# Two-layer transformer block on one core: normalisation by halves of the tokens, a new order of layer 1's first steps, and products on TensorE whose results nobody reads

## The reference

```python
x = L0_attn_x
xn = _layernorm(x, axis=-1)
s = _L0_attn_ref(xn, ...)          # 16 heads of 16, rope, degree-4 polynomial attention, out projection
g = _silu(_L0_ffn_ref(xn, ...))    # 4-bit weights unpacked, gate/up 2048, gelu, down
x = x + s * g
xn = _layernorm(x, axis=-1)
s = _L1_attn_ref(xn, ...)          # 16 q heads and 4 kv heads of 128, rope, alibi, capped softmax
g = _silu(_L1_ffn_ref(xn, ...))    # router, top 4 of 32 experts, one shared expert
x = x + s * g
```

## Time and profile before

| | before |
|---|---|
| three runs, us | 869.6, 869.14, 864.97 (median 869.14) |
| profiled execution, us | 866.74, its span 865.0 |
| busy: PE, DVE, ACT, POOL | 779.7 (90%), 612.7 (71%), 465.6 (54%), 422.8 (49%) |
| PE busy, in 40 slices of 21.6 us | 2999999988788758898999899999999999999996 |
| granted clock of PE in the same slices | 9999999999998989988999999999999999999999 |

### The profile page before, as it was taken

One profiled execution on the slowest core, in us unless ns is written; L12 is line 12 of the kernel. 1 busy time (PEld: TensorE's weight loads), 2 busy tenths in 40 slices (PEclk: granted clock), 3 DMA queues, 4 the chain that ended last, 5 costly groups with the idle time before them and its releaser, 6 DMA issues.

```text
span 865.0 us, 13854 instructions
## 1 busy us (share of the span) xinstructions
PE 779.7 (90%) x4835; PEld 635.0 (73%) x4835; DVE 612.7 (71%) x1063; ACT 465.6 (54%) x819; POOL 422.8 (49%) x478
## 2 busy tenths in 40 slices
PE   2999999988788758898999899999999999999996
PEld 2876776764223237687988788989999999988884
DVE  8388869547988868788877886767766654445555
ACT  3433342259888823676645556556566555655431
POOL 2566846423554454454433357577663412665430
PEclk9999999998989988999999999999999999999999
DMA  5111186000000040000000001110110569644107
GB/s 180 38 53 57 38 243 179 1 1 1 1 1 2 1 143 6 26 7 7 25 7 13 7 26 50 44 37 32 56 50 1 197 128 346 218 146 106 48 4 241
DMA packets 50115, 59.81 MB, mean 69 GB/s; under 512 B 13559, under 2 KB 41084, under 8 KB 50048
## 3 DMA queue, kind: packets, MB, share of 16 engines
q1 hardware_dynamic: 45488, 50.49, 19.2%
q0 software_dynamic: 4560, 8.44, 2.7%
HBM read 41.11 MB, written 21.86 MB: 73 GB/s over the span
## 4 chain that ended last, share of the span: by engine, by line
PE 56%; DVE 12%; POOL 6%; ACT 6%; issue 4%; DMA 1%; POOLq 0%; ACTq 0%; DVEq 0%; SPq 0%
PE ps L771 12%; PE ps L515 8%; PE ps L517 7%; PE ps L516 7%; PE ps L864 4%; PE ps L861 3%; PE ps L895 3%; POOL A L1735 2%; DVE cap L1442 2%; DVE swap L1432 2%; PE ps L609 2%; PE ps L554 2%; PE ps L843 2%; PE ps L686 2%; PE ps L780 1%
## 5 line engine op out<-in xcount | busy, mean ns | idle before, releaser
L1105 ACT ACTIVATE cap<-cap 128x1024 f32<-128x1024 f32 (+7 forms) x128 | 87.1, 680 | 123.1 <-DVE cap L1442 123.1
L771 PE MATMUL ps<-V,P 128*128 128x129 f32 x1152 | 152.6, 279 | 0.0
L771 PEld LDWEIGHTS ps<-V,P 128*128 128x128 f32 x1152 | 145.2, 194 | 2.7
L1442 DVE SCALAR_TENSOR_TENSOR cap<-dist,ps 128x1024 f32<-128x1024 f32 (+7 forms) x128 | 95.1, 749 | 26.2 <-PE ps L517 21.4
L1661 POOL TENSOR_SCALAR_AFFINE_SELECT P<-P 128x128 f32<-128x128 f32 x128 | 38.6, 301 | 148.8 <-ACT P L1110 148.5
L1791 POOL DMA_INDIRECT y_scratch<-y_sb,aux_s x63 | 62.0, 984 | 61.6 <-ACT y_sb L1150 40.3
L1110 ACT ACTIVATE P<-cap 128x1024 f32<-128x1024 f32 (+7 forms) x128 | 87.7, 685 | 4.1
L515 PE MATMUL ps<-q_hi,k_hi 128*128 128x512 f32 x192 | 72.1, 376 | 6.9 <-DVE cap L1442 6.2
L517 PE MATMUL ps<-q_lo,k_hi 128*128 128x512 f32 x192 | 67.0, 349 | 0.0
L516 PE MATMUL ps<-q_hi,k_lo 128*128 128x512 f32 x192 | 66.8, 348 | 0.0
L1766 POOL TENSOR_TENSOR rot<-rot,swap 128x512 f32<-128x512 f32 x40 | 52.1, 1304 | 19.7 <-DVE swap L1432 19.5
(11 more groups left out here) (288 smaller groups left out, 2099.2 us busy)
## 6 DMA issues: line engine op xcount, KB each, us to landing
xg_scratch<-blank SPq DMA_DIRECT2D x1, 8127.0 KB, 32.5
xa<-xg_scratch SPq DMA_DIRECT2D x63, 128.0 KB, 2.2
ew<-in_experts SPq DMA_DIRECT2D x3, 1920.0 KB, 8.7
y<-y_scratch SPq DMA_DIRECT2D x8, 512.0 KB, 5.4
pk<-in_packed SPq DMA_DIRECT2D x8, 384.0 KB, 3.2
pks<-in_scales SPq DMA_DIRECT2D x8, 384.0 KB, 4.0
ew<-in_experts SPq DMA_DIRECT2D x1, 3072.0 KB, 12.9
wqk<-in_wqk SPq DMA_DIRECT2D x20, 128.0 KB, 2.0
```

What stands on the lines that cost most here:

```text
L771: last = pe.matmul(ps[:, 4 + r % 2, o:o + D1 + 1], P1[:, h % 2, a:a + P], V1[:, j, h // REP, :], start=(j == 0), stop=(j == t))
L1105: act.activation(cap[:, n % 2, 0:w], cap[:, n % 2, 0:w], ACT.Tanh, scale=1.0 / (CAP * float(D1) ** 0.5))\
L1442: dve.scalar_tensor_tensor(out=cap[:, n % 2, 0:w], in0=dist[:, 0:w], scalar=slope, in1=psf[:, 1024 * (n % 2):1024 * (n % 2) + w], op0=ALU. ...
```

## The change

- Both layers: square root, `rsqrt`, shift and normalisation run for tiles 0 to 3, then for tiles 4 to 7. In each half DVE normalises two tiles and ACT two. `transpose_x`, `layernorm_hi` and `layernorm_lo` run by halves, in other PSUM banks.
- Layer 0: half 0 is normalised after the statistics of tile 4. wqkv is split by chunk on ACT and POOL, and POOL starts only after `shift_ready` of half 0. The second half's transposes stand between tiles 1 and 2 of `qkv0`; `nibbles(0, ...)` on DVE moves behind tile 0's copy, `halves(0)` behind tile 1's and the second half's low parts.
- Layer 1: DVE normalises half 0 between the statistics of tiles 4 and 5. POOL's `split_wqk(1)` and the router's split move behind wv's. The list begins: k0 half 0, values 0 and 1, the second half's transposes, q0 half 0, values 2 and 3, k0 half 1, q0 half 1, values 4 to 7. On ACT the high part of k0 half 0 comes after the second half's high parts.
- `keep_clock(n, bank)`: n products of x_tok with itself (128x128 by 128x256, 32-bit) into a bank that nobody reads. Eight once x's first half has landed, two after the first transposes of layer 0; six and two at the same places of layer 1.

```diff
+XT_BANKS = [(0, 2), (2 * PAIR_OF["turn_o", 1], OUT_BANKS[2])]
-            def transpose_x(layer):
-                for k in range(2 * NHALF):
-                    half, c = k // NC, k % NC
-                    pe.wait_ge(xn_ready if half == 0 else xn_act_ready, 4 * layer + 4)
+            def transpose_x(layer, half):
+                pe.wait_ge(xn_ready, 4 * layer + 2 * half + 2)
+                pe.wait_ge(xn_act_ready, 4 * layer + 2 * half + 2)
+                for c in range(NC):
                     for i in range(4):
...
             def qkv0():
-                pe.wait_ge(wqkv_ready, 1)
                 for t in range(NT):
+                    if t == 2:
+                        transpose_x(0, 1)
...
+                            if t == 0:
+                                pe.wait_ge(wqkv_ready, c + 1)
...
+            def keep_clock(n, bank):
+                for _ in range(n):
+                    pe.matmul(ps[:, bank, 0:D], x_tok[:, 0, 0:P], x_tok[:, 0, :], start=True, stop=True)
+
+            pe.wait_ge(in_x[0], 16)
+            keep_clock(8, 7)
             pe.wait_ge(in_const, 32)
-            transpose_x(0)
+            transpose_x(0, 0)
+            keep_clock(2, 7)
             qkv0()
...
-            pe.wait_ge(x_ready, NT)
-            transpose_x(1)
+            keep_clock(6, 2 * PAIR_OF["turn", H0 // QUAD - 1])
+            transpose_x(1, 0)
+            keep_clock(2, 2 * PAIR_OF["turn", H0 // QUAD - 1])
...
         def _(act):
...
+            layernorm_sd(0, 0)
             act.wait_ge(in_const, 32)
-            act.activation(wqkv_hi[:], wqkv[:], ACT.Copy).then_inc(wqkv_hi_ready, 1)
-            layernorm_sd(0)
-            layernorm_norm(0)
-            layernorm_hi(0)
+            split_wqkv(0)
+            layernorm_norm(0, 0)
+            split_wqkv(1)
+            layernorm_hi(0, 0)
+            layernorm_sd(0, 1)
+            layernorm_norm(0, 1)
             for t in range(NT):
+                if t == 2:
+                    layernorm_hi(0, 1)
...
             act.activation(rw_hi[:], rw[:], ACT.Copy).then_inc(rw_hi_ready, 1)
+            layernorm_sd(1, 0)
+            layernorm_norm(1, 0)
             act.wait_ge(in_wv, 16)
             act.wait_ge(so_ps, NT)
             act.activation(wv_hi, wv, ACT.Copy).then_inc(wv_hi_ready, 1)
-            layernorm_sd(1)
-            layernorm_norm(1)
-            layernorm_hi(1)
+            layernorm_hi(1, 0)
+            layernorm_sd(1, 1)
+            layernorm_norm(1, 1)
...
         def _(dve):
...
+            for t in range(NT):
+                if t % 4 == 0:
+                    dve.wait_ge(in_x[t // 4], 16)
+                tile_stats(t)
+                if t == 3:
+                    layernorm_var(0)
+                if t == 4:
+                    layernorm_norm(0, 0)
+            layernorm_lo(0, 0)
+            layernorm_var(1)
+            layernorm_norm(0, 1)
             for t in range(NT):
                 dve.wait_ge(qkv_ps, t + 1)
...
+                if t == 0:
+                    nibbles(0, 0)
+                    nibbles(0, 1)
+                if t == 1:
+                    layernorm_lo(0, 1)
+                    halves(0)
...
                 if t >= 1:
+                    dve.wait_ge(x_ready, t)
                     tile_stats(t - 1)
+                if t == 4:
+                    layernorm_var(0)
+                if t == 5:
+                    layernorm_norm(1, 0)
+            dve.wait_ge(x_ready, NT)
             tile_stats(NT - 1)
-            layernorm_stats(1)
-            layernorm_norm(1)
+            layernorm_lo(1, 0)
+            layernorm_var(1)
+            layernorm_norm(1, 1)
             dve.memset(V1[:, :, :, D1:D1 + 1], 1.0)
-            layernorm_lo(1)
...
         def _(pool):
...
-            pool.wait_ge(wqkv_hi_ready, 1)
-            pool.tensor_tensor(wqkv_lo[:], wqkv[:], wqkv_hi[:].bitcast(F32), ALU.subtract).then_inc(wqkv_ready, 1)
+            pool.wait_ge(shift_ready, 1)
+            for c in range(NC):
+                pool.wait_ge(wqkv_hi_ready, c + 1)
+                pool.tensor_tensor(wqkv_lo[:, c], wqkv[:, c], wqkv_hi[:, c].bitcast(F32), ALU.subtract).then_inc(wqkv_ready, 1)
...
-                if t in (1, 3):
-                    split_wqk(t // 2)
-                if t == 5:
-                    pool.wait_ge(rw_hi_ready, 1)
-                    pool.tensor_tensor(rw_lo[:], rw[:], rw_hi[:].bitcast(F32), ALU.subtract).then_inc(rw_ready, 1)
+                if t == 1:
+                    split_wqk(0)
             pool.wait_ge(wv_hi_ready, 1)
             pool.tensor_tensor(wv_lo, wv, wv_hi.bitcast(F32), ALU.subtract).then_inc(wv_ready, 1)
+            split_wqk(1)
+            pool.wait_ge(rw_hi_ready, 1)
+            pool.tensor_tensor(rw_lo[:], rw[:], rw_hi[:].bitcast(F32), ALU.subtract).then_inc(rw_ready, 1)
...
 def schedule():
...
+    steps += [("project", 0, 0), ("values", 0), ("values", 1), ("turn_x", 1, 1), ("project", first, 0), ("values", 2), ("values", 3)]
+    steps += [("project", 0, 1), ("project", first, 1)] + [("values", t) for t in range(4, NT)]
```

More of the change, by code:

```diff
@@ L932, in _, with layernorm_sd, layernorm_norm, layernorm_hi @@
         def _(act):
[L933 to L940, removed]
+            def layernorm_sd(layer, half):
+                act.wait_ge(var_ready, 3 * layer + half + 1)
+                h = slice(4 * half, 4 * half + 4)
+                act.activation(ln_sd[:, h], ln_var[:, h], ACT.Sqrt).then_inc(sd_ready, 1)
+            def layernorm_norm(layer, half):
+                act.wait_ge(shift_ready, 2 * layer + half + 1)
+                for t in (4 * half + 2, 4 * half + 3):
                     act.activation(xn_tok[:, t, :], x_tok[:, t, :], ACT.Identity, bias=ln_t[:, t:t + 1],
                                    scale=ln_r[:, t:t + 1]).then_inc(xn_act_ready, 1)
[L944 to L948, removed]
+            def layernorm_hi(layer, half):
+                for c in range(NC):
+                    act.wait_ge(xT_ps, 4 * layer + NC * half + c + 1)
+                    act.activation(xT_hi[:, c, half * HALF:(half + 1) * HALF], ps[:, XT_BANKS[layer][half] + c, :], ACT.Copy)\
                         .then_inc(xT_hi_ready, 1)
@@ L1205, in tile_stats, with layernorm_var @@
             def tile_stats(t):
-                dve.wait_ge(x_ready, t + 1)
                 link(dve.bn_stats(ln_stats[:, t % 2, :], x_tok[:, t, :]))
                 link(dve.bn_aggr(ln_mv[:, t, :], ln_stats[:, t % 2, :]))
[L1211 to L1215, removed]
+            def layernorm_var(half):
+                h = slice(4 * half, 4 * half + 4)
+                dve.tensor_scalar(ln_var[:, h], ln_mv[:, h, 1], LN_EPS, None, ALU.add).then_inc(var_ready, 1)
@@ L1216, in layernorm_norm @@
+            def layernorm_norm(layer, half):
+                h = slice(4 * half, 4 * half + 4)
+                dve.wait_ge(sd_ready, 3 * layer + half + 1)
+                rsqrt(ln_sd[:, h], ln_var[:, h], ln_r[:, h], ln_t[:, h])
+                dve.scalar_tensor_tensor(out=ln_t[:, h], in0=ln_mv[:, h, 0], scalar=-1.0, in1=ln_r[:, h], op0=ALU.mult,
                                          op1=ALU.mult).then_inc(shift_ready, 1)
-                for t in range(NT // 2):
+                for t in (4 * half, 4 * half + 1):
@@ L1218, in layernorm_norm, with layernorm_lo @@
                     dve.tensor_scalar(xn_tok[:, t, :], x_tok[:, t, :], ln_mv[:, t, 0:1], ln_r[:, t:t + 1],
                                       ALU.subtract, ALU.mult).then_inc(xn_ready, 1)
[L1221 to L1224 removed]
+            def layernorm_lo(layer, half):
+                for c in range(NC):
+                    dve.wait_ge(xT_hi_ready, 4 * layer + NC * half + c + 1)
@@ L1816, in schedule @@
     first = PROJ.index(("q", 0))
-    for i, n in enumerate(range(first + 1)):
-        steps += [("project", n, 0)] + [("values", 2 * i)] * i + [("values", 2 * i + 1)] * i
-        steps += [("project", n, 1)] + [("values", 0), ("values", 1)] * (i == 0)
-    steps += [("values", t) for t in range(4, NT)]
+    steps += [("project", 0, 0), ("values", 0), ("values", 1), ("turn_x", 1, 1), ("project", first, 0), ("values", 2), ("values", 3)]
+    steps += [("project", 0, 1), ("project", first, 1)] + [("values", t) for t in range(4, NT)]
     for h in range(H1 + 1):
@@ L1863, in follow @@
 def follow(engine):
-    out, later = [], []
+    out, later, held = [], [], []
     for n, s in enumerate(STEPS1):
@@ L1890, in follow @@
                 out.append(s)
-            if engine != "dve":
+            if engine == "act" and s == ("project", 0, 0):
+                held.append(("project_part", *s[1:]))
+            elif engine != "dve":
                 later.append(("project_part", *s[1:]))
@@ L1897, in follow @@
                 out.append(s)
+        elif name == "turn_x":
+            if engine != "pool":
+                out += [s] + held
         elif name in ("out", "logits", "turn_logits", "ranks", "values"):
```

50 lines of the change are left out of this document (21 added, 29 removed).

## The result

The changed kernel takes 856.54 us (854.07 to 858.26, four runs) where the kernel before takes 868.59 beside it: ratio 0.9876, 95% interval 0.9845 to 0.9907. Measured twice more, on two chips (e2, e12), it gives 0.988 (0.9847 to 0.9914) and 0.987 (0.9837 to 0.9903). By the ratios that is 10 to 11 us off (the two medians above are 12.1 apart). I had forecast 861.5, from a sum of -5.75. The profiled execution took 856.94 us, its span 855.2.

A forecast was written before the change was run, and what follows sets the result against it. PE was taken to bound most of the span, other engines and the clock sharing elsewhere. Layer 0's -3.85 and layer 1's -1.9 sum to -5.75, from the profiled 866.74 to 861.0; forecast 861.5 us, range 856 to 867.

The forecast's parts named there:

- my 3.85: Layer 0's start in all: the lead less inserted work and clock loss gives -3.85 us, between -5.5 and -2.
- `qkv0`'s start: Layer 0: normalising and transposing by halves lets `qkv0` start at 14.3 instead of 20.25, -5.95 us.
- What is put into `qkv0`: Layer 0: eight transposes between `qkv0`'s tiles cost +0.9 us, a stall of PE at tile 6 +0.2.
- The clock, +1.0: Layer 0: `qkv0` may begin at 1.2 GHz after broken work, losing 0 to 2.0 us, taken as +1.0.
- Layer 1, first projection: Layer 1's entry: the first projection starts at 325.5 instead of 330.45, 5 us sooner.
- Layer 1, scores, -1.9: Layer 1: lead mostly lost on DVE; head 0's scores start at 346.4, -1.9 us, bounds -3.5 to +1.
- the -3.5: Layer 1: DVE's first rope step starts at 328.7 instead of 332.22, -3.5 us.
- Rival A: Both starts: filler keeps 2.4 GHz and layer 1's lead reaches the scores, giving 858.2 us; chance 0.13.
- B: Layer 1: DVE's queue takes all the lead, +0 to +1 us there, giving 863.4; chance 0.17.
- C: Layer 0: late `halves(0)` and ACT's queue stall PE at tile 6, giving 862.8 or 865 us; chance 0.11.
- D: Layer 0, 203 to 306 us: clock falls meet other work, ending level at 866.7 or slower at 870.7; chance 0.05.

The follow-up runs named there:

- e2: The changed kernel run again without any edit, for a second profile: 859.71 us, ratio 0.988 to the kernel before.
- e12: The changed kernel run a third time without any edit: 859.31 us against 870.01 for the kernel before, ratio 0.987.
- e4: The changed kernel with POOL's low part of wqkv waiting for xn_ready instead of shift_ready: 858.67 us, ratio 0.9871 to the kernel before.
- e1: The kernel before, run again without any edit for a second profile: 871.18 us against 870.32, ratio 1.001.
- e9: The changed kernel with 4 useless products instead of 8 at the start and 3 instead of 6 in layer 1: 860.67 us, ratio 0.989 to the kernel before.
- e3: The changed kernel without any keep_clock products: 865.99 us, ratio 0.9956 to the kernel before.
- e8: The changed kernel with POOL waiting for xn_ready in layer 0 and another list order at layer 1's start: 857.1 us, ratio 0.9893 to the kernel before.
- e10: The kernel of e8 with further useless products in layer 0's attention: 861.06 us against 857.92 without them.
- e11: The same kernel as e8, measured again beside the changed kernel: 857.92 us, ratio 0.9851 to the kernel before.
- e6: The kernel before with only layer 1's part of the change, layer 0 starting as before without filler: 862.23 us, ratio 0.9947.
- e5: The kernel before with only layer 0's part of the change, layer 1 as before without filler: 859.15 us, ratio 0.9921.
- e7: The kernel before with useless products alone, 21 at layer 0's start and 17 behind its out projection: 863.49 us, ratio 0.9977.

## Why the prediction was right in sign and range, and where its steps failed

The time, 856.54, lies in my range of 856 to 867, by half a microsecond, and the gain is 10 to 11 us where my sum has 5.75. That it lies inside owes something to luck. I kept near the profiled 866.74, where the four measurements of before have medians of 867.85 to 870.32; from the one beside the changed kernel, 868.59, the same sum gives 862.8, farther off. And in layer 0 the first pair's 4.02 matches my 3.85 only because errors cancel: `qkv0` began 0.7 later than I had it, and the clock cost nothing where I had put 1.0.

- **`qkv0`'s start, -5.95.** In the three profiles it is 15.02, 14.79 and 13.73 against my 14.3, -5.2 to -6.5. The step that the wait on `shift_ready` frees DVE was right for `rsqrt` (0.16) and wrong for what follows: I let the two normalisations run beside POOL's first instruction, and in two of the three the second was held 1.5 to 1.6 us by it. I had named that as a way to be wrong. The Trainium skill (SBUF — State Buffer, § Who interferes with whom) names `tensor_scalar` among the operations that can take the ports that DVE and GpSimd share. By the Trainium skill (SBUF — State Buffer, § Who interferes with whom) whichever issues first has them for its whole instruction, and the other is blocked that long. e4 and the rows of the race agree: in the first profile the held pair ended at 11.74, just after POOL's first instruction (11.59).
- **What is put into `qkv0`, +0.9 and +0.2.** From its first matmul to gate/up 19.09 us pass in the changed kernel and 17.88 before, +1.2. ACT's wait for POOL before tile 4's copy (1.42) and the late pair of copies are the 0.2 to 0.3.
- **The clock, +1.0, was the failed step.** Its term is 0 in the changed kernel, whose `qkv0` starts at full speed, and it is negative against the kernel before: e1's `qkv0` took 18.77, 0.9 more than the first profile's, so before the change too the start sometimes lies ahead of the clock's rise. I priced a useless product from a transpose by its columns, 0.45 us, eight of them until 8.5. It is two instructions (x16), and eight took 5.45 us until 10.34, so the gap before the transposes was 1.5 us and not 2.5. The page of the kernel before already had a row to tell me: L771 counts 1152 matmuls for 576 products of 32 bits. With my length, e9, the clock did fall. I gave the clock 0 to 2.0 us in layer 0 and nothing in layer 1, where a low clock was to be covered by DVE; without the filler (e3) the two places lose 3.0 and 1.9.
- **Layer 1, first projection.** From wout's first use it came 3.65 sooner (18.24 to 14.59), not 5. The clock goes with the rest: it was low at wout in all three profiles of the changed kernel, where e8, e10 and e11, with the same program up to there and a full clock, need 13.34 to 13.36, 4.9 less than before. I had taken that stage from before, where it ran at the full clock. PE's windows from wout's first use on, of the changed kernel, then of e8:

```profile
306.00:308.00 2.00, 2.00 (x11) 0.50 1.03 412
```
```profile
306.00:308.00 2.00, 1.50 (x12) 1.00 0.94 298
```

- **Layer 1, scores, -1.9.** DVE's first rope step came 3.05 sooner (17.16 after wout against 20.21), near the -3.5, and POOL then stood between the parts, as reckoned (1.18 and 0.61). In the first pair the scores gain 1.2, a full clock before against a low one after. Low clock against low clock (e1's 38.60, the changed kernel's 35.1) it is 3.5; so my term was small by up to 1.6.
- **Rival A** (the clock holds), to which I gave 0.13, had the mechanism that came in layer 0, and its 858.2 is the nearest of my cases. In layer 1 the clock held from the filler on, but was low at wout. **B** (DVE's queue takes all) took part of the lead only; **C** showed as 0.2 to 0.3 us. **D**'s longer attention stretch did not come: it is 99.3 to 101.2 in the changed kernel and 100.6 to 102.3 before.

**What stays open.** In the mean of the profiles the edited stretches give 5.0 (38.13, 38.85, e6's 38.24 against 34.11, 33.85, 32.80, e5's 32.84) and 2.0 to 3.5 us, together 7 to 8.5. The three ratios say 10 to 11, with intervals that begin at 7.5 to 8.4. Outside the two stretches the span holds 790.6, 792.3 and 785.8 us in before, e1 and e7, and 786.0, 792.5 and 792.0 in after, e2 and e12: no gain shows there, but either kind scatters by 6.5. So whether the other 2 to 4 us are chance or lie in the unedited stretches, the runs do not settle.

## What to carry to other kernels

Moving work forward to the moment its data is ready gives its full lead only if TensorE's clock is up by then (10 to 11 us with the filler here, 3.8 without); look at whether the engine rests just before it, and fill that rest up to the last moment with products nobody waits for. Price such a product by a row of its own kind, operand type included, and expect nothing from it where the engine rests for less than a microsecond inside a chain (e10). When a wait is set so that two engines just miss each other, take the event after the last instruction that shares the resource: here that is `xn_ready` and not `shift_ready`.

## What the runs showed that I had not expected

- A DVE `tensor_scalar` with its scalars in SBUF, 128x256, was held by a POOL `tensor_tensor` that began at about the same time or up to 0.1 us before it (pair 2.31, 2.27, 2.22 us) and not by one that began some 0.2 us later (0.73). Its free speed, 0.33 a tile, had looked to me like that of an operation that shares nothing.
- A 32-bit 128x128 by 128x256 product is two matmul instructions and took 0.44 us at 2.4 GHz (17 in 7.50) and 0.88 at 1.2 GHz (four in 3.50).
- The changed kernel's three profiles have mean granted clocks of 0.980, 0.976 and 0.970, which is about 34, 41 and 52 us of the span at 1.2 GHz, and its attention stretch is 99.3, 101.2 and 101.1 us in them.
